# A graph layer and an LSTM layer on one core: the first 10,000 edges as products of summed weights with 80 support rows kept in SBUF, and ten gathered tiles a place instead of twelve

## The chip, the core and the metric

One NeuronCore of a Trainium2 chip runs the whole program. Its engines are TensorE (PE, with its weight loads shown as PEld), VectorE (DVE), ScalarE (ACT), GpSimd (POOL) and SyncE (SP), and 16 DMA engines move data between HBM and SBUF. Each engine works through its own queue in order, and they wait for each other on semaphores. The metric is the device time of one execution in microseconds, and less is better.

## What is computed

Two residual layers follow each other on x, 6250 nodes by 256 features. The first is a graph layer over 100,000 edges (sorted by `dst`), and the second is an LSTM over the nodes, with a gated sum over the nodes behind it.

```python
support  = einsum('ni,oi->no', layernorm(x), W_weight) + W_bias     # 6250 x 256
messages = support[dst] * edge_weight[:, None]                      # 100000 x 256
x = x + segment_sum(messages, src, num_segments=6250)
h = lstm(layernorm(x))                                              # one sequence of 6250 steps, 256 wide
w = argmax(h @ W_lin.T + b_lin) * h;  inc = cumsum(w)
x = x + 2.0 * h + (inc - w) * fw_att + (inc[-1] - inc) * bw_att
```

`dst` is drawn as 6250 times the square of a uniform number and then sorted, so small values are frequent and stand first: the first 10,000 edges name support rows 0 to 60 alone. `src` is uniform.

## The kernel before

**The layout.** The nodes are cut into 125 segments (`SEGS`) of 50 nodes (`SEGL`). A *place* is a position inside a segment, so one step of the LSTM handles 125 nodes at once, one of each segment. The first half of the program sorts the edges by place, computes `support`, and stores it in HBM as `support_scratch`. The sorted edges form *tiles* of 128 edges that belong to one place. A tile costs three operations:

- GpSimd gathers the 128 support rows of the tile from HBM with one indirect DMA into a slot of `ring` (a part of `big_a`), in `gather_place` (L573), by row numbers that ACT copied to `stg_g`.
- VectorE writes the tile's one-hot matrix, 128 edges by 125 segments with the edge weight in it, in `onehot` (L1180), four tiles ahead.
- TensorE multiplies the two into one of four PSUM banks, in `place_tile` (L1793), and VectorE adds the bank onto the place's rows of x, in `add_tile` (L1186). Which rows these are comes from `table`, whose entries `blocks` loads into registers of VectorE's sequencer (L1189).

**The stages.** 224 tiles are done while the edges are still being sorted (up to about 600 us of the profile). The other tiles are done in the *place stage*. It is a row of *turns* that each engine runs through as `place(it, q)`. Turn h = 2·it + q does `PACE` = 12 tiles, scales place h - 3 (layer norm), and runs the LSTM step for place h - 4. Tiles are in turns 2 to 50 (49 x 12 = 588 = `RUN`), and turns 51 and 52 have none. Then the LSTM runs alone (L1825, the same recurrence again from a better start), with the output sums beside it.

**The order inside a turn** is written out by hand on each engine. TensorE does tiles 0 and 1, then tiles 2 to 5 each behind a quarter of the 32 input projections (`project_input`, L1812), then tiles 6 to 9 with the 32 products of the recurrence between them (`product`, L1819), then tiles 10 and 11, then two transposes of the next scaled input (L1801). The profile shows an fp32 product of this size as two instructions, so a quarter is 8 matmul rows. VectorE does, for each tile n, `hot(n)` (the one-hot of tile n + 4) and `add(n)`, with the pieces of the layer norm (L1256 to L1320) and of the cell between them: `products` (L1327, L1329), `state` (L1335), `hidden` (L1340). It loads six table entries before tile 0 and six behind tile 5.

**What holds back what.** A product waits for its gather, for its one-hot, and for the addition four tiles back, which frees its PSUM bank. A gather waits, once in four (`PARTIAL`), for the product eight tiles back (`LOOK`). An addition waits for its product.

Of the kernel before, what the change touches and what calls it, by code (L numbers as in the profile page):

```python
# [6 lines left out]
P = 128  # L7
# [8 lines left out]
CC = 20  # L16
# [9 lines left out]
TILES = (EP * CC * CHUNKS + NB * (P - 1)) // P  # L26
# [3 lines left out]
RUN = 588  # L30
REST = TIL[1] - RUN
TMAX = max(TIL)
RECS = tuple(-(-t // P) for t in TIL)
RROWS = -(-(TILES * P // BLK + GRP * P) // P) * P
# [4 lines left out]
PACE = 12  # L39
WIDE = 2 * PACE  # L40
AHEAD = 4
HOTS = 8
PSR = 4
# [3 lines left out]
LAG, FIRST = 3, 2  # L47
# [14 lines left out]
INDEX_AT = 400  # L62
EPS = 1e-5
# [3 lines left out]
def build(nc, A, out, slow_sweeps=SEGS, tol=TOL):  # L67
# [14 lines left out]
    with ExitStack() as ctx:  # L82
# [15 lines left out]
        chunk_c = sb("chunk_consts", [CHUNKS, 5 * CHUNKS + 2])  # L98
        earlier, first, both, half, col_pair = (chunk_c[:, i * CHUNKS:(i + 1) * CHUNKS] for i in range(5))
        first_p = chunk_c[:, 5 * CHUNKS:5 * CHUNKS + 1]  # L100
        my_pair = chunk_c[:, 5 * CHUNKS + 1:5 * CHUNKS + 2]
# [109 lines left out]
        rect = at(flat_a, 11136, P, -(-TMAX // P), 2 * P)  # L211
        spread = at(flat_c, 1024, CHUNKS, SUPERS, 2, BB)
# [71 lines left out]
        gat = [sem(f"gathered{i}") for i in range(RING)]  # L284
        gat2 = [sem(f"gathered_by_place{i}") for i in range(WIDE)]
# [50 lines left out]
        o_v = sem("outputs_done")  # L336
        segt = sem("segment_totals_ready")
# [51 lines left out]
        def _(sp):  # L389

            def load_edges_of(tile, name, loaded):
                for a, b in PARTS:
                    sp.dma_start(tile[a:b, :], A[name].rearrange("(p c) -> p c", p=EP)[a:b, :]).then_inc(loaded, 16)
# [42 lines left out]

            def store_pair(i, to):
# [53 lines left out]
        def _(pool):  # L491
# [130 lines left out]
        def _(act):  # L622
# [179 lines left out]
            def place(it, q, w=0):  # L802
# [3 lines left out]
                if h > LAG + 1:  # L806
                    tanh_c(u - 1, 1 - q, 1)
# [1228 lines left out]
```

## Time and profile before

| | |
|---|---|
| three timed runs | 1674.13, 1678.54 and 1686.15 us, median 1678.54 |
| the profiled execution, its own span | 1678.9 us |
| busy in it: PE, PEld, DVE, ACT, POOL | 83%, 72%, 78%, 37%, 66% |
| mean granted TensorE clock | 0.945 |
| place stage (first to last addition of turns 2 to 50) | 604.72 to 1338.84 us |
| indirect gathers: of tiles before the place stage, of places | 224, 588 |

In a row of the trace an instruction group is shown as engine, line, operation, written tile, read tiles and count. A number in brackets is the time in which the engine stood idle before it, with what ended that. "issue" there is time in which the engine waited for nothing that the profile shows. The completion of a gather is often not seen as a releaser, and a wait for it then counts as "issue".

### The profile page before, as it was taken

What the parts mean: (1) busy time and instruction counts of PE and PEld (TensorE: products, weight loads), DVE (VectorE), ACT (ScalarE), POOL (GpSimd) and SP (SyncE); (2) the same over time, 40 slices, a digit from 0 to 9 for tenths busy, and PEclk for the clock granted to TensorE, in tenths of its full rate; (3) what the DMA queues carried; (4) which work ended last, traced back from release to release, by engine and by line L of the source; (5) the groups of instructions that cost most, each with busy time, mean ns of one, the idle gap of its engine ahead of it and who ended that gap; (6) DMA issues with size and microseconds to landing.
All of it is one profiled execution on the core that took longest, in us unless ns stands there. A gap on an engine that the chain in (4) does not pass through costs nothing.

```text
span 1678.9 us, 35611 instructions
## 1 busy us (share of the span) xinstructions
PE 1396.6 (83%) x9305; PEld 1206.7 (72%) x9305; DVE 1305.0 (78%) x3956; ACT 625.7 (37%) x2098; POOL 1101.8 (66%) x1165
## 2 busy tenths in 40 slices
PE   6688767877787759888889888888888889999991
PEld 3557665666676638777777777777777788999991
DVE  8799959999999867777777777777777744666666
ACT  0626630000000003333334333333433467777770
POOL 0226637777777777777777777777777600588884
PEclk9799977999999969999999999999999999999996
DMA  9211113334333334444444444444444334444434
GB/s 223 54 49 42 22 17 100 89 87 138 95 88 87 88 100 130 137 146 129 153 131 129 153 128 153 130 128 153 129 138 144 116 126 122 125 124 119 119 110 154
DMA packets 64189, 193.28 MB, mean 115 GB/s; under 512 B 21473, under 2 KB 22853, under 8 KB 63261
## 3 DMA queue, kind: packets, MB, share of 16 engines
q0 software_dynamic: 45232, 108.65, 23.6%
q1 hardware_dynamic: 18904, 84.00, 15.9%
q8 instruction: 23, 0.38, 0.1%
q14 instruction: 30, 0.25, 0.0%
HBM read 151.39 MB, written 41.04 MB: 115 GB/s over the span
## 4 chain that ended last, share of the span: by engine, by line
PE 51%; DVE 14%; issue 12%; DVEq 5%; ACT 1%; POOL 1%; DMA 1%; ACTq 0%; POOLq 0%
PE bank L1825 13%; PE bank L1793 13%; PE bank L1812 8%; PE bank L1750 5%; PE bank L1819 5%; PE bank L1719 5%; DVE big_c L1180 3%; DVE big_a L1129 3%; DVEq L1189 3%; DVE big_b L1186 2%; DVEq L1180 1%; DVE big_a L1535 1%; DVE big_a L1124 1%; PE bank L1855 1%; PE bank L1856 1%
## 5 line engine op out<-in xcount | busy, mean ns | idle before, releaser
L573 POOL DMA_INDIRECT big_a<-support_scratch,stg_g x588 | 563.0, 958 | 180.5 <-issue 143.3
L1793 PE MATMUL bank<-big_a,big_c 128*125 128x256 f32 x1176 | 362.9, 398 | 86.6 <-issue 58.3
L1186 DVE TENSOR_TENSOR big_b<-big_b,bank 125x256 f32 x812 | 338.8, 417 | 93.2 <-PE bank L1793 80.8
L1180 DVE TENSOR_SCALAR big_c<-consts_sb,listed 128x125 f32<-128x125 f32 x812 | 296.5, 366 | 37.1 <-issue 19.9
L1793 PEld LDWEIGHTS bank<-big_a,big_c 128*125 128x125 f32 x1176 | 180.5, 191 | 146.2 <-DVE big_c L1180 83.4
L527 POOL DMA_INDIRECT big_a<-support_scratch,stg_g x224 | 214.3, 957 | 73.6 <-issue 56.2
L1825 PE MATMUL bank<-big_c 128*128 128x125 f32 x2048 | 256.9, 280 | 4.6 <-DVE big_c L1340 4.6
L1825 PEld LDWEIGHTS bank<-big_c 128*128 128x128 f32 x2048 | 241.3, 191 | 15.5 <-issue 7.2
L1812 PEld LDWEIGHTS bank<-xt,w_ih 128*128 128x128 f32 x1600 | 207.9, 192 | 15.9 <-ACT xt L634 3.7
L1819 PEld LDWEIGHTS bank<-big_c 128*128 128x128 f32 x1600 | 209.0, 192 | 10.8 <-ACT bank L748 0.5
L1812 PE MATMUL bank<-xt,w_ih 128*128 128x125 f32 x1600 | 210.3, 275 | 2.6 <-ACT xt L634 2.5
L1819 PE MATMUL bank<-big_c 128*128 128x125 f32 x1600 | 209.8, 275 | 0.1
L1750 PE MATMUL bank<-big_a,big_c 128*125 128x256 f32 x448 | 139.9, 448 | 75.1 <-DVE big_b L1186 67.0
L1719 PEld LDWEIGHTS bank<-big_a,big_c 125*128 125x128 f32 x1480 | 184.6, 205 | 21.3 <-DVE big_a L1129 10.1
L1719 PE MATMUL bank<-big_a,big_c 125*128 125x128 f32 x1480 | 184.3, 287 | 16.3 <-DVE big_a L1129 8.4
L1750 PEld LDWEIGHTS bank<-big_a,big_c 128*125 128x125 f32 x448 | 85.4, 213 | 118.9 <-DVE big_c L1180 82.5
L740 ACT ACTIVATE pr<-bank,gate_bias 128x125 f32<-128x125 f32 x400 | 113.3, 367 | 89.1 <-PE bank L1812 88.3
L787 ACT ACTIVATE big_c<-big_c 128x125 f32<-128x125 f32 x228 | 70.3, 309 | 164.8 <-DVE big_c L1335 162.4
L508 POOL TENSOR_TENSOR pr<-pr,b_gnn 125x256 f32<-125x256 f32 x50 | 61.5, 1249 | 102.8 <-ACT pr L644 102.8
L694 ACT CAST stg_g<-listed 128x12 uint32 (+3 forms) x77 | 14.4, 190 | 302.0 <-PE bank L1750 238.4
L780 ACT ACTIVATE big_c<-bank 128x250 f32<-128x250 f32 x100 | 38.0, 380 | 225.3 <-PE bank L1819 225.3
L590 POOL TENSOR_TENSOR listed<-listed 125x256 f32<-125x256 f32 x50 | 36.5, 729 | 125.0 <-DVE listed L1472 124.8
(272 smaller groups left out, 1982.3 us busy)
## 6 DMA issues: line engine op xcount, KB each, us to landing
big_c<-gate_input_scratch SPq DMA_DIRECT2D x64, 508.0 KB, 3.6
gate_input_scratch<-pr SPq DMA_DIRECT2D x25, 1016.0 KB, 4.6
big_a<-support_scratch,stg_g POOLq DMA_INDIRECT x812, 2.8
support_scratch<-pr SPq DMA_DIRECT2D x12, 448.0 KB
big_b<-in_x SPq DMA_DIRECT2D x2, 1904.0 KB
out<-big_a SPq DMA_DIRECT2D x2, 1456.0 KB
big_b<-in_x SPq DMA_DIRECT2D x1, 1792.0 KB
out<-big_a SPq DMA_DIRECT2D x1, 1344.0 KB
```

The lines of the kernel that those rows point to most:

```text
L527: pool.indirect_dma_start(out=ring[:, s, :], out_offset=None, in_=sup_d, in_offset=bass.IndirectOffsetOnAxis(ap=stg_g[:, q, j:j + 1], axis ...
L573: pool.indirect_dma_start(out=ring[:, s, :], out_offset=None, in_=sup_d, in_offset=bass.IndirectOffsetOnAxis(ap=stg_g[:, q, n:n + 1], axis ...
L740: ins = nc.scalar.activation(gate_in[q][:, 4 * x + c, 2:XW], bank[2 + x][:, c * SEGS:(c + 1) * SEGS], ACT.Identity, bias=bias[:, 4 * x + c ...
L787: nc.scalar.activation(act_c[:, x, :], c_s[:, 1 - q, x, :], ACT.Tanh).then_inc(a_c[x], 1)
L1180: V.tensor_scalar(oneh[:, s % HOTS, 0:SEGS], iota[:, 0:SEGS], src_of[:, ds(t, 1)], w_of[:, ds(t, 1)], ALU.is_equal, ALU.mult).then_inc(oh_ ...
L1186: V.tensor_tensor(at, at, bank[4 + s % PSR][0:SEGS, 0:D], ALU.add).then_inc(added, 1)
L1719: ins = mm(bank[b][:, 0:2 * NPOS], slots_home(k, q)[:, c, :], col_v[:, q, c, :, :].rearrange("p v n -> p (v n)"), start=q == 0 and c == 0, ...
L1750: mm(bank[4 + s % PSR][0:SEGS, 0:D], oneh[:, s % HOTS, 0:SEGS], ring[:, s % RING, :], start=True, stop=True).then_inc(prod, 1)
L1793: mm(bank[4 + s % PSR][0:SEGS, 0:D], oneh[:, s % HOTS, 0:SEGS], ring[:, s, :], start=True, stop=True).then_inc(prod, 1)
L1812: ins = mm(bank[2 + x][:, c * SEGS:(c + 1) * SEGS], w_ih[:, k, g:g + P], xt[:, q, k, 0:SEGS], start=k == 0, stop=k == 1)
L1819: return mm(bank[b + x][:, c * SEGS:(c + 1) * SEGS], w_hh[:, k, g:g + P], h_s[:, q, k, :], start=False, stop=True, skip_group_check=True)
L1825: return mm(home, w_hh[:, k, g:g + P], h_s[:, q, k, :], start=False, stop=True, skip_group_check=True)
```

## The change

The edges are laid out anew, so that the first 10,000 of them fill the last four of the 40 chunks that are sorted. They get two tiles of 128 records for each place (`HOTP` = 2), and these 100 tiles are never gathered. The 80 first rows of `support` (`hot_sup`) are loaded into SBUF once. In each turn TensorE multiplies, for both tiles, a one-hot by support row (128 x 80, `hot_dst_1`) with a weighted one-hot by segment (128 x 125, `hot_seg_1`) and sums them in bank 5 (`sum_weights`). ACT copies the 80 x 125 sums to `hot_sum`, TensorE multiplies them with `hot_sup` into bank 4 (`hot_product`), and VectorE adds the result (`add_sum`). VectorE writes the four one-hots for a turn in the turn before (`next_sum`). The remaining edges fill 528 tiles of places, 510 of which are reserved for places with ten a turn, so turns 1 to 51 have tiles. What was a short repair for tiles that are left over has become a full second path that runs when a flag is set; it is also set if a place has more than 256 of the first edges or one of them names a row over 79.

```diff
-RUN = 588
+RUN = 510
-PACE = 12
+PACE = 10
-LAG, FIRST = 3, 2
+HELD = 5
+LAG, FIRST = 3, 1
+POSITION = (0, 2, 3, 4, 5, 6, 7, 9, 10, 11)
+ADDS_BEFORE = (-3, -1, 0, 1, None, 2, 3, 5, 6, 7)
...
+act.wait_ge(sum_p, g + 1)
+nc.scalar.copy(hot_sum[:, 0:SEGS], bank[5][0:HOTROWS, 0:SEGS]).then_inc(sum_r, 1)
...
+def add_sum():
+    dve.wait_ge(hot_pr, g + 1)
+    dve.wait_ge(added, before_us + 7)
+    V.tensor_tensor(at, at, bank[4][0:SEGS, 0:D], ALU.add).then_inc(added, 1)
...
+def hot_onehot(g, r, i, of):
+    if of == 0:
+        V.tensor_scalar(hot_seg_1[:, r, i, 0:SEGS], iota[:, 0:SEGS], hot_seg[:, ds(g * HOTP + i, 1)],
+                        hot_w[:, ds(g * HOTP + i, 1)], ALU.is_equal, ALU.mult)
+    else:
+        ins = V.tensor_scalar(hot_dst_1[:, r, i, :], iota[:, 0:HOTROWS], hot_dst[:, ds(g * HOTP + i, 1)], None,
+                              ALU.is_equal)
+        if i == HOTP - 1:
+            ins.then_inc(hot_r, 1)
...
+def sum_weights(g, r):
+    pe.wait_ge(hot_r, g + 1)
+    for i in range(HOTP):
+        ins = mm(bank[5][0:HOTROWS, 0:SEGS], hot_dst_1[:, r, i, :], hot_seg_1[:, r, i, 0:SEGS],
+                 start=i == 0, stop=i == HOTP - 1)
+    ins.then_inc(sum_p, 1)
+def hot_product(g):
+    pe.wait_ge(sum_r, g + 1)
+    mm(bank[4][0:SEGS, 0:D], hot_sum[:, 0:SEGS], hot_sup, start=True, stop=True).then_inc(hot_pr, 1)
...
 tile_of(0)
+sum_weights(g, r)
+if stepping:
+    project_input(u, q, 0, (0, 1))
 tile_of(1)
```

**TensorE at the start of a turn in the loop, before.** The rows are tile 0 (it multiplies `big_c`, the one-hot, with `big_a`, the gathered rows), tile 1, the first quarter of the projections (`w_ih`), and tile 2.

```order
L1791 REGISTER_ALU [waits onehot_ready]
L1793 MATMUL bank<-big_a,big_c 125x256 [waits tile_added,gathered_by_place0]
L1790 REGISTER_ALU
L1793 MATMUL bank<-big_a,big_c 125x256 [waits tile_added,gathered_by_place1,onehot_ready]
L1806 ISA
L1808 REGISTER_ALU [waits transposed2_ready]
L1812 MATMUL bank<-xt,w_ih 128x125 [waits gate_input_ready0]
L1812 MATMUL bank<-xt,w_ih 128x125 x3
L1790 REGISTER_ALU
L1793 MATMUL bank<-big_a,big_c 125x256 [waits tile_added,gathered_by_place2,onehot_ready]
```

The same place after the change:

```order
L1936 MATMUL bank<-big_a,big_c 125x256 [waits tile_added]
L1944 REGISTER_ALU [waits hot_onehots_ready]
L1946 MATMUL bank<-big_c 80x125 [waits tile_added]
L1946 MATMUL bank<-big_c 80x125
L1967 REGISTER_ALU
L1969 REGISTER_ALU [waits transposed2_ready]
L1973 MATMUL bank<-xt,w_ih 128x125 [waits gate_input_ready0]
L1973 MATMUL bank<-xt,w_ih 128x125 x3
L1929 REGISTER_ALU
L1935 REGISTER_ALU [waits gathered11,onehot_ready]
L1936 MATMUL bank<-big_a,big_c 125x256 [waits tile_added]
```

The two products of the weight sums (L1946) stand between tile 0 and all projections of the turn, behind a wait for `hot_onehots_ready`. Tile 1 now comes behind the first quarter of the projections.

**VectorE at the end of a turn, before.** The rows are the last one-hot and addition, `hidden` of the first half, and `products` of the second half; the next turn starts with the table load.

```order
L1335 TENSOR_TENSOR big_c<-big_c 128x125 [waits state_products_ready0]
L1180 ISA [waits tile_product_done]
L1180 TENSOR_SCALAR big_c<-consts_sb,listed 128x125
L1184 REGISTER_ALU
L1186 ISA [waits tile_added,tile_product_done]
L1186 TENSOR_TENSOR big_b<-big_b,bank 125x256
L1340 TENSOR_TENSOR big_c<-big_c 128x125 [waits tanh_c_done0]
L1327 TENSOR_TENSOR big_c<-big_c 128x125 [waits act_i_f_done1]
L1329 TENSOR_TENSOR big_c<-big_c 128x125 [waits tanh_g_done1]
L1189 ISA
L1189 TENSOR_LOAD table
```

The same place after the change:

```order
L1415 TENSOR_TENSOR big_c<-big_c 128x125 [waits state_products_ready0]
L1445 REGISTER_ALU
L1446 REGISTER_ALU [waits tile_product_done]
L1448 ISA [waits tile_added]
L1448 TENSOR_TENSOR big_b<-big_b,bank 125x256
L1543 ISA
L1543 TENSOR_SCALAR big_c<-consts_sb,big_c 128x125
L1420 TENSOR_TENSOR big_c<-big_c 128x125 [waits tanh_c_done0]
L1546 ISA
L1546 TENSOR_SCALAR big_c<-consts_sb,big_c 128x80
L1407 TENSOR_TENSOR big_c<-big_c 128x125 [waits act_i_f_done1]
L1409 TENSOR_TENSOR big_c<-big_c 128x125 [waits tanh_g_done1]
```

The last one-hot of the weight sums for the next turn (L1546, 128x80), which counts `hot_onehots_ready` up, is the third last instruction of VectorE's turn.

## Rows read from the trace of the kernel before

**Rows 1.** Windows: from:to, length, busy us (instructions) of each engine, clock, DMA.

```profile
0.00:603.00 603.00, 450.57 (x2573) 360.81 (x2573) 543.43 (x895) 128.13 (x397) 362.31 (x333) 0.89 0.33 84
...
655.00:1335.00 680.00, 601.73 (x4044) 526.90 (x4045) 509.19 (x2162) 262.71 (x898) 515.93 (x539) 1.00 0.44 138
```

**Rows 2.** Lines, 655 to 1335 us: group, count | busy, mean | idle before.

```profile
L573 POOL DMA_INDIRECT big_a<-support_scratch,stg_g x539 | 516.1, 957 | 164.3 <-issue 130.2 <-PE bank L1793 32.0 <-ACT stg_g L694 2.1
L1793 PE MATMUL bank<-big_a,big_c 128*125 128x256 f32 x1080 | 329.1, 392 | 78.6 <-issue 55.1 <-DVE big_c L1180 22.3
L1186 DVE TENSOR_TENSOR big_b<-big_b,bank 125x256 f32 x540 | 225.4, 417 | 75.7 <-PE bank L1793 72.3 <-issue 0.3
```

**Rows 3.** Timeline, TensorE in two turns: start us, us, group, idle before.

```profile
1049.68 0.67 PE L1793 MATMUL bank<-big_a,big_c 128*125 128x256 f32 x2 [1.48 <-issue]
...
1056.78 0.60 PE L1793 MATMUL bank<-big_a,big_c 128*125 128x256 f32 x2
1057.21 1.05 PE L1812 MATMUL bank<-xt,w_ih 128*128 128x125 f32 x8
1058.10 0.60 PE L1793 MATMUL bank<-big_a,big_c 128*125 128x256 f32 x2
```

**Rows 4.** Timeline, VectorE in the same two turns.

```profile
1050.48 0.42 DVE L1186 TENSOR_TENSOR big_b<-big_b,bank 125x256 f32 x1 [1.68 <-PE bank L1793]
...
1054.52 0.35 DVE L1180 TENSOR_SCALAR big_c<-consts_sb,listed 128x125 f32<-128x125 f32 x1 [0.90 <-issue]
...
1058.36 0.42 DVE L1186 TENSOR_TENSOR big_b<-big_b,bank 125x256 f32 x1
...
1059.22 0.42 DVE L1186 TENSOR_TENSOR big_b<-big_b,bank 125x256 f32 x1
1061.13 0.15 DVE L1302 TENSOR_SCALAR rstd<-sums 125x1 int32<-125x1 int32 x1 [1.49 <-issue]
...
1065.72 0.27 DVE L1335 TENSOR_TENSOR big_c<-big_c 128x125 f32<-128x125 f32 x1
1065.92 0.33 DVE L1180 TENSOR_SCALAR big_c<-consts_sb,listed 128x125 f32<-128x125 f32 x1
1066.17 0.40 DVE L1186 TENSOR_TENSOR big_b<-big_b,bank 125x256 f32 x1
1066.51 0.27 DVE L1340 TENSOR_TENSOR big_c<-big_c 128x125 f32<-128x125 f32 x1
1066.70 0.27 DVE L1327 TENSOR_TENSOR big_c<-big_c 128x125 f32<-128x125 f32 x1
...
1067.67 0.35 DVE L1180 TENSOR_SCALAR big_c<-consts_sb,listed 128x125 f32<-128x125 f32 x1 [0.50 <-PE bank L1793]
```

**Rows 5.** Timeline, LSTM stage: a write by VectorE, the product behind it.

```profile
1449.45 0.29 DVE L1340 TENSOR_TENSOR big_c<-bank,big_c 128x125 f32<-128x125 f32 x1 [0.37 <-ACT big_c L787]
...
1449.95 4.00 PE L1825 MATMUL bank<-big_c 128*128 128x125 f32 x32
```

**Rows 6.** Line L1189, the table load, whole program: ns min/median/max, first, last.

```profile
L1189 DVEq TENSOR_LOAD <-table x126: 594/810/2470, 257.7 to 1331.6; - x126
```

**Rows 7.** Chain of waits, the load behind tile 5: start us, us.

```profile
1043.85 1.41 DVEq L1189
```

**Rows 8.** Timeline, VectorE: first addition of turns 2, 3, 4, last of all.

```profile
604.72 0.42 DVE L1186 TENSOR_TENSOR big_b<-big_b,bank 125x256 f32 x1 [0.41 <-PE bank L1793]
...
614.71 0.41 DVE L1186 TENSOR_TENSOR big_b<-big_b,bank 125x256 f32 x1
...
628.79 0.41 DVE L1186 TENSOR_TENSOR big_b<-big_b,bank 125x256 f32 x1
...
1338.84 0.42 DVE L1186 TENSOR_TENSOR big_b<-big_b,bank 125x256 f32 x1 [0.40 <-PE bank L1793]
```

**Rows 9.** Timeline, TensorE in the turns without tiles: their projections.

```profile
1348.36 3.84 PE L1812 MATMUL bank<-xt,w_ih 128*128 128x125 f32 x32 [1.04 <-ACT xt L634]
...
1357.33 3.84 PE L1812 MATMUL bank<-xt,w_ih 128*128 128x125 f32 x32 [1.04 <-ACT xt L634]
```

More of the change, by code:

```diff
@@ L97, in build @@
         ident, iota, before, shift, ones = (consts[:, i, :] for i in range(5))
[L98 to L101, printed above, removed]
+        chunk_c = sb("chunk_consts", [CHUNKS, 6 * CHUNKS + 5 + 2 * BB])
+        earlier, first, both, half, col_pair, cold = (chunk_c[:, i * CHUNKS:(i + 1) * CHUNKS] for i in range(6))
+        first_p, my_pair, cold_p, hot_p, over = (chunk_c[:, 6 * CHUNKS + i:6 * CHUNKS + i + 1] for i in range(5))
+        hot_at, hot_n = (chunk_c[:, 6 * CHUNKS + 5 + i * BB:6 * CHUNKS + 5 + (i + 1) * BB] for i in range(2))
         number_i = sb("pair_numbers_i", [CHUNKS, CHUNKS + 1], i32)
@@ L283, in build @@
         gst = sem("gather_rows_staged")
-        gat = [sem(f"gathered{i}") for i in range(RING)]
-        gat2 = [sem(f"gathered_by_place{i}") for i in range(WIDE)]
+        gat = [sem(f"gathered{i}") for i in range(WIDE)]
         ln2 = sem("place_scale_steps")
@@ L435, in _ @@
                 sp.dma_start(tile[:, :, :], A[name].rearrange("(k p) f -> p k f", p=P)).then_inc(load_w, 16)
+            sp.wait_ge(scat, scattered(SUPERS))
+            sp.dma_start(rect_hot, rec_tiles[HOTAT:HOTAT + HOTT, :]).then_inc(rec_hot, 16)
+            for q in range(2):
+                sp.wait_ge(st0[q], SUPPORT_STORES[q])
+            sp.dma_start(hot_sup, sup_d[0:HOTROWS, :]).then_inc(load_hot, 16)
             def store_pair(i, to):
@@ L1449, in _ @@
                     place(it, q, SEGL - LEAD)
-            for q in range(2):
-                place(turning, q)
-            with dve.Fori(turning + 1, ENDING) as it:
+            for it in range(turning, turned_to + 1):
+                for q in range(2):
+                    place(it, q)
+            with dve.Fori(turned_to + 1, ENDING) as it:
                 for q in range(2):
@@ L1661, in _ @@
             mm(bank[2][0:CHUNKS, P // 2:P // 2 + BB], first, cnt, start=True, stop=True)
-            mm(bank[2][0:CHUNKS, P:P + BB], ones[0:CHUNKS, 0:CHUNKS], cnt, start=True, stop=True)
+            mm(bank[2][0:CHUNKS, P:P + BB], cold, cnt, start=True, stop=True)
             mm(bank[2][0:CHUNKS, 2 * P:2 * P + BB], both, cnt, start=True, stop=True)
```

291 lines of the change are left out of this document (207 added, 84 removed).

## The prediction

> **What bounds the kernel now.** I read the stages first, then the waits in the long one. The edges are sorted until about 603 us, and the change touches little there. The place stage runs from the first addition of turn 2 at 604.72 to the last addition at 1338.84 [rows 8]. In 680 us of it PE is busy 602 us, DVE 509, POOL 516, ACT 263, with the TensorE clock at its full level, 1.00 of 2.4 GHz [rows 1]. None of these shares is 100%, so it is the pace that tells. GpSimd makes 539 gathers in these 680 us, 516.1 busy and 164.3 idle, and 130.2 of the idle time is "issue", which is no wait for another engine [rows 2]. One gather thus takes (516.1 + 164.3) / 539 = 1.262 us, and 12 take 15.15 us, a turn. Only 34 us of its idle time, 0.06 us a gather, are waits for PE and ACT. TensorE waits 55.1 us for something that the profile does not show [rows 2]; the gap of 1.48 us in front of one tile's product is such a wait [rows 3], and a gather that had not landed fits it. VectorE waits 72.3 us for these products [rows 2]. Now the place stage goes at the pace of the gathers.
>
> How fast would the others be without that? In the turn from 1054.52 to 1067.67 VectorE waits for no product, apart from 0.50 us at its end that coincide with a table load: 13.15 us for 12 tiles [rows 4]. TensorE's minimum is smaller. A tile takes 1057.21 - 1056.78 = 0.43 us and a quarter of the projections 0.89 us (to the next tile at 1058.10), and the recurrence has four such parts as well [rows 3]. That makes 12 x 0.43 + 8 x 0.89 + 0.22 for the transposes (as two of the 8 in a quarter) = 12.5 us.
>
> **The change, engine by engine, a turn.** GpSimd: two gathers less, 10 x 1.262 = 12.6 us. TensorE: two tiles less (-0.87), the product with `hot_sup` (+0.43, one of a tile's size), and the weight sums, half the rows of a quarter (+0.44): 12.5 us as before. ScalarE: one copy more, on an engine busy 263 of 680 us [rows 1]. The trace has no such copy alone; between nothing and 0.5 us it is hidden, since the sums are wanted only by tile 4, four projections later. VectorE: a one-hot costs 1066.17 - 1065.92 = 0.25 us, an addition 1066.51 - 1066.17 = 0.34 [rows 4]. Two of each go (-1.18), one addition and four one-hots come (+1.34): 13.3 us.
>
> So by throughput a turn would fall to 13.3 us. **But the change also closes a chain.** TensorE's products of the weight sums stand in front of all projections of a turn and wait for a one-hot that VectorE writes as the third last instruction of the turn before. Queued behind that wait are the projections and tiles 1 to 4, and VectorE can't pass its addition of tile 4 without them. I go once round, with t = 0 where VectorE starts that last one-hot:
>
> - VectorE to TensorE: in the LSTM stage the product at 1449.95 follows the write it waited for, started at 1449.45, by 0.50 us [rows 5].
> - Weight sums 0.44, first quarter 0.89, then three steps of tile and quarter, 1.32 each (1056.78 to 1058.10) [rows 3]: tile 4 starts at 0.50 + 0.44 + 0.89 + 3.96 = 5.79.
> - Its addition starts 0.80 later, as the addition at 1050.48 does behind the product at 1049.68 [rows 3, 4]: 6.59.
> - VectorE from there. Before, from the addition of tile 4 at 1058.36 to `state` at 1065.72 it takes 7.36 us [rows 4]. After, the same stretch holds one addition less (-0.34), one one-hot less (-0.25) and two one-hots of the sums more (+0.50): 7.27. The table load is in both: 1.91 us from the addition at 1059.22 to 1061.13, of which the load is 1.41 [rows 4, 7]. It now stands behind tile 4.
> - From `state` to the last one-hot: 0.20, an addition 0.34, a one-hot 0.25, `hidden` 0.19 (1066.51 to 1066.70) [rows 4]: 0.98.
>
> Together 6.59 + 7.27 + 0.98 = 14.84 us a turn. VectorE's own way from t to the addition of tile 4 is shorter: 1058.36 - 1054.52 = 3.84, plus 0.97 from 1066.70 to 1067.67 and 0.25, 5.1 us [rows 4]. So it waits some 1.5 us a turn for tiles 3 and 4, and TensorE stands about 2.3 us in front of the weight sums. What goes away as a wait for gathers comes back here. 14.84 exceeds 13.3, 12.6 and 12.5, so it sets the turn.
>
> **The load's size is the unknown in it.** Before, six entries are loaded, from an even place in the table; after, five, half of the loads from an odd one. The trace has nothing of that shape. Its loads take from 0.59 us upwards with a median of 0.81, and 1.41 behind tile 5 [rows 6, 7]. I keep 1.41, the row from the same spot. At 0.6 the turn would be 14.0 us; if the new start costs as much more as lies between 0.81 and 1.41, 15.4 us. The Trainium skill ("DMA: Bandwidth & Descriptors", Latency and other measured facts) puts the floor of a `tensor_load` at about 600 ns. By that floor alone the turn would be 14.0 us and the time about 1645 us; the shortest loads here agree, the ones behind tile 5 do not.
>
> **The sum**, against the profiled 1678.9 us, which is the median of the three runs (1678.5) to within 0.4 us:
>
> - Turns 5 to 50, 46 of them: 14.84 for 15.15, -14.3.
> - Turn 51 gets tiles: 14.84 for the 8.97 us of a turn without them (1348.36 to 1357.33) [rows 9], +5.9.
> - Turn 1 is new. Turn 2, which has tiles alone, takes 614.71 - 604.72 = 10.0 us [rows 8]; with two tiles less and the sums' work more, by the prices above +0.16, about 10.1.
> - Turns 2 to 4: +0.1 in turn 2. Turn 3 takes 628.79 - 614.71 = 14.1 now [rows 8], with gathers as its pace; without that, 10.1 and the layer norm, some 12.5, -1.6. Turn 4 I take at 14.3 for 15.1, -0.8. Together -2.3.
> - Ahead of turn 1: some 15 small operations more on VectorE, each waiting for the one in front. Such an operation costs between 0.15 and 0.3 us (the smallest in a row lasts 0.15 [rows 4]), and some are hidden; then six to unpack the new records, four more one-hots (1.0), and a third transfer in front of the first operation. Bounds 1.5 and 7; I take 4.5.
>
> -14.3 + 5.9 + 10.1 - 2.3 + 4.5 = +3.9, so 1683 us. Every 0.1 us in the turn is 4.7 us here.
>
> **The rivals.**
>
> - *No chain, VectorE's throughput sets the pace*: 13.3 us a turn, 47 x 1.54 = 72 less, 1611 us. For it: the products of the sums are small, and some slack may be hidden from me, if the stretch of VectorE shortens. Against it: the order of both queues, which fixes every step above. The Trainium skill ("Perfetto Trace Analysis", Identifying the Most-Contended Engine) would have the most occupied engine relieved first, and by occupancy TensorE is that here, which the change does not relieve.
> - *Chain with cheap loads*: at 0.6 us a load 14.0 us a turn, 47 x 0.81 = 38 less, 1645 us. For it, the shortest and the median load; against it, the place in the table.
> - *The other side, dearer loads*: if a start at an odd entry costs 0.6 us more, 15.4 us a turn, 1711 us. It decides from 15.1 us, +0.27 in a turn, since there the time is 1% over. For it: the load behind tile 5 is dearer than the one at a turn's start, though both take six entries, so the start or the surroundings count.
> - *The gathers still pace*, since 10 take 12.6: it would give no less than VectorE's 13.3 and no more than 14.84, so the chain hides it.
> - *The change does not do what it says*: with the second path the time would be several times longer. Counted from the inputs, a place has at most 237 of the first edges (256 fit), they name rows up to 60 (80 fit), and the cold tiles of each place end at least four tiles within the limit. Under 1 in 100.
>
> **How the numbers follow.** The likeliest case is the chain at 14.5 to 15.1 us, with 0.5: 1667 to 1696 us, 1683 in its middle. Dearer loads or other extra steps on the chain 0.22, cheap loads 0.13, no chain 0.13, the rest 0.02. The range has to hold 8 in 10: it takes in the cheap loads and the dearer ones, 1640 to 1712, and leaves out the case without a chain. Under about 1% a measurement of this kernel can't be told from no change, so the bounds are 1662 and 1695. Faster: 0.26 from the two quick cases and a little of the main one, 0.28. Slower: 0.22 and the upper end of the main one, 0.27. Same: 0.45.
>
> **What would show it.** Right: additions evenly 14.8 us a turn apart; TensorE idle some 2 us in front of the products of the weight sums, released by VectorE's last one-hot (80 wide); VectorE waiting for the products of tiles 3 and 4; no gather late, and GpSimd waiting for TensorE some 2 us a turn. The load behind tile 4 shows its size directly. Wrong: weight sums that start without a gap, a turn near 13.3 us, or gaps of TensorE of the "issue" kind in front of gathered tiles.

## The result, and the profile after

The changed kernel takes 1661.5 us, the median of four runs (1658.7 to 1662.8). The kernel before took 1677.6 us beside it (four runs, 1674.1 to 1686.2). The ratio is 0.990, with a 95% interval from 0.987 to 0.993. So the change saves 16 us, 1.0%; the interval leaves out 1, so it is a gain, if a small one. The forecast was 1683 us, slightly more than before. The time lies in the range from 1640 to 1712, but the sign was wrong.

The profiled execution of the kernel after has a span of 1658.7 us, against 1678.9 before. These are 600 us of its place stage (window, its length, PE, PEld, DVE, ACT and POOL busy with their numbers of instructions, then the granted clock, the DMA share and GB/s).

```profile
700.00:1300.00 600.00, 538.77 (x3816) 485.36 (x3814) 476.29 (x2040) 245.26 (x871) 401.02 (x418) 1.00 0.41 128
```

GpSimd has become the engine with time to spare: 67% busy, where it was 76% in [rows 1]. TensorE's share has hardly risen, 90% for 88%. The groups of instructions of the same stretch answer to [rows 2]: busy time and mean ns of one, then the idle time in front of them and what ended it.

```profile
L630 POOL DMA_INDIRECT big_a<-support_scratch,stg_g x418 | 401.9, 962 | 199.3 <-issue 108.3 <-PE bank L1936 82.8 <-ACT stg_g L753 8.2
L1936 PE MATMUL bank<-big_a,big_c 128*125 128x256 f32 x830 | 238.0, 385 | 4.6 <-DVE big_b L1448 3.1 <-issue 1.5
L1448 DVE TENSOR_TENSOR big_b<-big_b,bank 125x256 f32 x415 | 173.6, 418 | 41.8 <-PE bank L1936 37.6 <-issue 0.2
L1946 PE MATMUL bank<-big_c 128*80 128x125 f32 x164 | 26.6, 285 | 55.2 <-DVE big_c L1546 55.2
```

No gathered tile comes late any more: the "issue" time in front of TensorE's tiles, 55.1 us before [rows 2], is 1.5 us. GpSimd waits 82.8 us for TensorE, 2.0 us a turn. In return TensorE waits 55.2 us in front of the weight sums (L1946), in each of the 41 turns of the stretch, for VectorE's 80-wide one-hot (L1546). The forecast named exactly this wait, but at 2.3 us a turn, where it is 1.35. Here is the turn on TensorE:

```profile
996.47 0.65 PE L1946 MATMUL bank<-big_c 128*80 128x125 f32 x4 [1.54 <-DVE big_c L1546]
996.96 1.06 PE L1973 MATMUL bank<-xt,w_ih 128*128 128x125 f32 x8
...
1007.54 1.03 PE L1936 MATMUL bank<-big_a,big_c 128*125 128x256 f32 x4
...
1010.90 0.65 PE L1946 MATMUL bank<-big_c 128*80 128x125 f32 x4 [1.12 <-DVE big_c L1546]
```

and on VectorE (start, duration; L1448 adds a tile, L1367 is the first operation behind the table load, L1415 is `state`, L1546 writes the 80-wide one-hots):

```profile
1001.33 0.42 DVE L1448 TENSOR_TENSOR big_b<-big_b,bank 125x256 f32 x1 [0.46 <-PE bank L1936]
...
1002.64 0.42 DVE L1448 TENSOR_TENSOR big_b<-big_b,bank 125x256 f32 x1 [0.44 <-PE bank L1936]
1004.22 0.15 DVE L1367 TENSOR_SCALAR tmp<-sums 125x1 f32<-125x1 f32 x1 [1.16 <-issue]
...
1008.37 0.42 DVE L1448 TENSOR_TENSOR big_b<-big_b,bank 125x256 f32 x1
...
1009.53 0.28 DVE L1415 TENSOR_TENSOR big_c<-big_c 128x125 f32<-128x125 f32 x1
...
1010.51 0.26 DVE L1546 TENSOR_SCALAR big_c<-consts_sb,big_c 128x80 f32<-128x80 f32 x1
```

From one L1946 to the next is 1010.90 - 996.47 = 14.43 us, and the turns of the stretch are even. VectorE waits in front of tiles 3 and 4, as foreseen (0.90 us here, 1.5 in the forecast). What is not as foreseen is the length, 14.43 us and not 14.84.

### The profile page after: what moved, and what is told of

Read it like the earlier page. It is cut to its first block, busy times and chain, and to the rows that moved or that the text cites. A ratio compares the mean times of both kernels' runs of the same rounds, so it can differ in the third digit from the quotient of the medians.

```text
span 1658.7 us, 36173 instructions
## 1 busy us (share of the span) xinstructions
PE 1387.2 (84%) x9451; PEld 1213.6 (73%) x9451; DVE 1328.6 (80%) x4070; ACT 630.2 (38%) x2150; POOL 1027.9 (62%) x1087
## 4 chain that ended last, share of the span: by engine, by line
PE 51%; DVE 17%; issue 8%; DVEq 5%; POOL 1%; ACT 1%; DMA 1%; POOLq 0%; ACTq 0%
PE bank L1986 13%; PE bank L1973 11%; PE bank L1936 8%; PE bank L1888 5%; PE bank L1980 5%; PE bank L1851 4%; DVE big_b L1448 3%; DVE big_a L1204 3%; DVEq L1264 2%; PE bank L1946 2%; DVE big_c L1546 1%; DVE big_c L1407 1%; DVE big_a L1665 1%; DVE big_c L1420 1%; DVE big_a L1199 1%
## 5 line engine op out<-in xcount | busy, mean ns | idle before, releaser
L630 POOL DMA_INDIRECT big_a<-support_scratch,stg_g x510 | 490.1, 961 | 232.9 <-issue 131.4
L1936 PE MATMUL bank<-big_a,big_c 128*125 128x256 f32 x1020 | 296.2, 391 | 9.2 <-DVE big_b L1448 5.0
L583 POOL DMA_INDIRECT big_a<-support_scratch,stg_g x224 | 213.9, 955 | 75.7 <-issue 57.3
L1448 DVE TENSOR_TENSOR big_b<-big_b,bank 125x256 f32 x510 | 213.3, 418 | 55.4 <-PE bank L1936 50.6
L1536 DVE TENSOR_SCALAR big_c<-consts_sb,listed 128x125 f32<-128x125 f32 x510 | 180.3, 354 | 40.7 <-issue 35.4
L1888 PE MATMUL bank<-big_a,big_c 128*125 128x256 f32 x448 | 140.3, 449 | 77.8 <-DVE big_b L1261 68.7
L1851 PE MATMUL bank<-big_a,big_c 125*128 125x128 f32 x1480 | 182.8, 286 | 16.3 <-DVE big_a L1204 8.4
L1936 PEld LDWEIGHTS bank<-big_a,big_c 128*125 128x125 f32 x1020 | 163.2, 192 | 28.9 <-DVE big_b L1448 9.7
L1888 PEld LDWEIGHTS bank<-big_a,big_c 128*125 128x125 f32 x448 | 85.1, 213 | 122.2 <-DVE big_c L1255 86.7
L846 ACT ACTIVATE big_c<-big_c 128x125 f32<-128x125 f32 x228 | 70.3, 308 | 222.1 <-DVE big_c L1415 219.8
L753 ACT CAST stg_g<-listed 128x10 uint32 (+3 forms) x79 | 14.8, 189 | 298.3 <-PE bank L1888 242.3
L1261 DVE TENSOR_TENSOR big_b<-big_b,bank 125x256 f32 x224 | 93.2, 416 | 8.4 <-PE bank L1888 8.0
```

The source lines that it names most:

```text
L583: pool.indirect_dma_start(out=ring[:, s, :], out_offset=None, in_=sup_d, in_offset=bass.IndirectOffsetOnAxis(ap=stg_g[:, q, j:j + 1], axis ...
L630: pool.indirect_dma_start(out=ring[:, s, :], out_offset=None, in_=sup_d, in_offset=bass.IndirectOffsetOnAxis(ap=stg_g[:, r, n:n + 1], axis ...
L1261: V.tensor_tensor(at, at, bank[4 + s % PSR][0:SEGS, 0:D], ALU.add).then_inc(added, 1)
L1448: V.tensor_tensor(at, at, bank[4 + POSITION[n] % PSR][0:SEGS, 0:D], ALU.add).then_inc(added, 1)
L1536: V.tensor_scalar(oneh[:, s % HELD, 0:SEGS], iota[:, 0:SEGS], src_of[:, ds(t, 1)], w_of[:, ds(t, 1)], ALU.is_equal, ALU.mult).then_inc(oh_ ...
L1851: ins = mm(bank[b][:, 0:2 * NPOS], slots_home(k, q)[:, c, :], col_v[:, q, c, :, :].rearrange("p v n -> p (v n)"), start=q == 0 and c == 0, ...
```

## The experiments

Each kernel was run four times, ten times where its size was unsteady or small, and once where only loads are looked at. The kernel before, run beside them, took 1677.9 to 1680.2 us. Turns are counted between the additions of the sums, as their mean from 700 to 1300 us of the profiled execution, or to the end of the place stage where that comes sooner.

### Three of the one-hots earlier: is the chain there?

```
 better_guess(j, p, 0)
 next_sum(0, 0)
+next_sum(0, 1)
+next_sum(1, 0)
+next_sum(1, 1)
...
 hot(9)
-next_sum(0, 1)
...
 add(9, vals)
-next_sum(1, 0)
...
     hidden(u, q, 0)
-next_sum(1, 1)
```

> The changed kernel with the other three one-hots of the next place's sums moved up beside the first of them, ahead of the addition of the sums (some 4 us earlier in VectorE's order); the work is the same. Theory (a chain from the last of them through TensorE's weight sums, tiles 1 to 4 and back sets the turn): the chain opens, TensorE's idle time of 1.1 to 1.5 us in front of the weight sums goes, and the turn falls from 14.45 to VectorE's own 13.2 to 13.6 us, its waits for tiles 3 and 4 taken off. 47 turns by 0.85 to 1.25 is 40 to 59 us: 1603 to 1622 us. Rival (a turn is as long as the work on TensorE or VectorE, the order does not count): within 5 us of 1661.

Measured: 1637.3 us, 24 less than after; ratio to before 0.976 (0.974 to 0.978). The same work in another order gains, so order counts, and the wait in front of the weight sums is gone. But a turn takes 13.91 us in the mean, and not 13.2 to 13.6, and the time misses the 1603 to 1622 us expected. The next wait is in TensorE's rows, at the projections (L1972):

```profile
996.72 1.15 PE L1972 MATMUL bank<-xt,w_ih 128*128 128x125 f32 x8
...
1008.95 0.43 PE L1961 MATMUL bank<-consts_sb,xn 125*128 125x125 f32 x2 [0.52 <-DVE xn L1400]
...
1010.73 1.16 PE L1972 MATMUL bank<-xt,w_ih 128*128 128x125 f32 x8 [0.38 <-ACT xt L693]
```

and in ScalarE's rows of the same moment, the tanh of the cell state (L846) and behind it the copy of the input (L693):

```profile
1010.11 0.31 ACT L846 ACTIVATE big_c<-big_c 128x125 f32<-128x125 f32 x1 [1.80 <-DVE big_c L1415]
1010.33 0.35 ACT L693 COPY xt<-bank 128x250 f32<-128x250 f32 x1
```

The wait of 0.52 us in front of the transposes (L1961) does not count in this turn, since TensorE waits again behind it. The copy was ready to be made earlier, but it stands in ScalarE's queue behind a tanh that waits for VectorE's `state`. So there is a third way round: projections, tile 4, its addition, the table load, `state`, tanh, copy, projections. It takes 14.01 us here.

### The table aligned: what does the load cost, and is it on the path?

```
+link(V.tensor_copy(spaced_t[0:1, 0:16 * RUN // 10].rearrange("p (x e) -> p x e", e=8)[:, :, 0:5],
+                   table[0:1, TFROM[1]:TFROM[1] + RUN].rearrange("p (x e) -> p x e", e=5)))
...
-return blocks(first + (TFROM[1] + n), PACE // 2) if n < count else None
+return blocks(g * 16 + n // 5 * 8, PACE // 2, spaced_t) if n < count else None
```

> The changed kernel with the table of places copied once into groups of 8 words with five used, so that every load of five entries begins at a multiple of 8. If the start in the table is what makes a load take 1.18 us and not 0.60, both loads of each turn take 0.60. The chain goes through the one behind tile 4, so the turn is 14.45 - 0.58 = 13.87 us and the time 47 x 0.58 = 27 us less, about 1634. If the place of the load in the program makes it dear (a load behind tile 4 and not its start), nothing changes: 1661. If loads are cheaper but the turn does not follow, the chain is wrong.

The loads of the kernel after, and of this one (least, median and greatest ns):

```profile
L1264 DVEq TENSOR_LOAD <-table x84: 586/1183/1210, 699.6 to 1299.8; - x84
```

```profile
L1265 DVEq TENSOR_LOAD <-table_by_places x83: 585/590/601, 701.1 to 1294.5; - x83
```

Every load now takes 0.59 us, so the start in the table makes it dear and not its place in the program. Yet the time is 1664.2 us (ratio to before 0.991, 0.988 to 0.994) and the turn 14.48 us: nothing is gained. (The copy of the table is not what hides a gain: VectorE spends 0.4 us on it, ahead of the stage, and the turn itself is no shorter.) VectorE now waits at other tiles. These are the additions of tiles 7 and 8:

```profile
1000.79 0.42 DVE L1449 TENSOR_TENSOR big_b<-big_b,bank 125x256 f32 x1 [0.27 <-PE bank L1939]
...
1002.11 0.42 DVE L1449 TENSOR_TENSOR big_b<-big_b,bank 125x256 f32 x1 [0.25 <-PE bank L1939]
```

So what I expected if the turn didn't follow, "the chain is wrong", is too short: the chain is real, but a second one stands beside it. From the weight sums on TensorE has no gap until tile 8, 1007.54 - 996.47 = 11.07 us in the kernel after. The addition of tile 8 can start 0.80 us later, VectorE goes from it to the last one-hot in 1010.51 - 1008.37 = 2.14 us, and TensorE follows 0.39 us behind: 14.40 us. In the kernel after the two ways, through tile 4 with the load and through tile 8 without it, differ by 0.03 us. To shorten one brings nothing. Moving the one-hots cuts both, since both end in them.

### Three more one-hots, ahead of the last one or behind it

```
+aside = sb("one_hots_aside", [P, 3, HOTROWS])
...
+if summing:
+    for n in range(3):
+        V.tensor_scalar(aside[:, n, :], iota[:, 0:HOTROWS], hot_dst[:, ds(g * HOTP, 1)], None, ALU.is_equal)
 next_sum(1, 1)
```

That is the one with the three ahead. In the other the same lines stand behind `next_sum(1, 1)`.

> The changed kernel with three more 80-wide one-hots a turn on VectorE (0.17 us each, written to a spare place, read by nobody) directly ahead of the last one-hot of the sums. Theory of the chain: all 0.51 us lie on it, 47 turns by 0.51 is +24 us, 1685. Rival (throughput of VectorE): also +24.

> The same three one-hots directly behind the last one-hot of the sums instead of ahead of it. Theory of the chain: they lie beside TensorE's weight sums and first projections, where VectorE later waits some 0.9 us for tiles 3 and 4, so they are covered: within 3 us of 1661, and these waits get shorter by 0.5 us in all. Rival (throughput of VectorE): +24 us, 1685, as with the three ahead.

Behind it, they cost nothing: 1660.4 us, with VectorE busy for 20 us more in the stretch (496.75 for 476.29):

```profile
700.00:1300.00 600.00, 541.38 (x3815) 485.08 (x3814) 496.75 (x2165) 244.93 (x870) 397.51 (x418) 1.00 0.41 128
```

I had expected the waits for tiles to cover all of these 20 us, and they cover a part. VectorE's idle time in front of its additions that ends with a product falls from 37.6 to 32.7 us, and most of the rest goes from the idle time in front of the tiles' one-hots, 30.8 us in the kernel after and 16.0 here.

Ahead of it, the same three cost 91 us: 1752.9 us, and not the 24 expected. This pair is the clearest proof of the chain, since only the place differs. The size has a second cause. A few turns take 14.9 to 15.0 us, which is 14.43 + 0.51 as the chain has it, but most take 16.5 to 17.0. TensorE's rows at two turns, both behind a wait for the last one-hot (L1550):

```profile
1013.06 0.65 PE L1950 MATMUL bank<-big_c 128*80 128x125 f32 x4 [1.93 <-DVE big_c L1550]
1013.54 1.06 PE L1977 MATMUL bank<-xt,w_ih 128*128 128x125 f32 x8
...
1045.12 1.01 PE L1950 MATMUL bank<-big_c 128*80 128x125 f32 x4 [2.23 <-DVE big_c L1550]
1045.92 1.91 PE L1977 MATMUL bank<-xt,w_ih 128*128 128x125 f32 x8
1047.63 1.06 PE L1940 MATMUL bank<-big_a,big_c 128*125 128x256 f32 x2
```

The same eight products take 1.06 us in one turn and 1.91 in the other. The stretches of these moments show why (the third number from the end is the granted clock):

```profile
1014.00:1016.00 2.00, 2.00 (x18) 1.92 (x17) 1.31 (x6) 0.55 (x3) 0.18 (x1) 1.00 0.17 51
...
1046.00:1048.00 2.00, 2.00 (x10) 1.96 (x10) 0.33 (x2) 0.56 (x3) 0.00 (x0) 0.50 0.07 27
...
1050.00:1052.00 2.00, 2.00 (x19) 1.95 (x17) 1.39 (x7) 1.46 (x5) 1.39 (x3) 1.00 0.23 66
```

Behind 2.23 us of idleness the clock is at its lower level, 1.2 GHz, and the path stretches by 1.5 to 2 us until it is back. The Trainium skill ("TensorE: Matmul & The Clock Gate", What's actually happening) says that the reduced clock is the default and that activity lifts it; this trace agrees, with the clock at 0.50 behind the idle time and at 1.00 again later in the same turn.

### One more one-hot ahead

```
+aside = sb("one_hots_aside", [P, 3, HOTROWS])
...
+if summing:
+    V.tensor_scalar(aside[:, 0, :], iota[:, 0:HOTROWS], hot_dst[:, ds(g * HOTP, 1)], None, ALU.is_equal)
 next_sum(1, 1)
```

> The changed kernel with one more 80-wide one-hot (0.17 us) directly ahead of the last one-hot of the sums, where three made turns of 14.95 us at TensorE's full clock and of 16.5 to 16.9 us with it at its lower level behind the longer gap. Theory (the chain sets the turn, and the clock is what made three cost 92 us): the gap in front of the weight sums stays near that of the changed kernel, the clock stays at its full level, and the turn is 14.43 + 0.17 = 14.60: 47 x 0.17 = 8 us, 1669. Rival (an operation there costs in proportion to what three cost): +31, 1692.

Measured: 1674.5 us, the median of ten runs that lie far apart (1669.6 to 1689.5). The lowest of them are what the chain gives, 1669. The profiled execution is the longest of the ten, and it shows both in one:

```profile
700.00:1000.00 300.00, 267.78 (x1905) 242.21 (x1905) 236.37 (x1023) 123.20 (x433) 201.01 (x205) 1.00 0.40 124
1040.00:1300.00 260.00, 231.69 (x1552) 208.14 (x1551) 196.29 (x843) 100.78 (x354) 160.03 (x170) 0.95 0.39 122
```

From 730 to 1020 us most turns are 14.60, to the hundredth what 14.43 + 0.17 makes. From then on many take 16.3 us, with the clock at the lower level behind the wait. The length of the wait in front alone does not decide it: 1.3 us was followed by the lower clock in some turns of this kernel, and in the kernel with the aligned table waits of up to 1.86 us were all followed by the full one. So 0.2 us a turn on top of the kernel after is enough for TensorE's idle time to cost more than itself in some executions. What exactly sets the edge stays open.

### Two more gathers, and the kernel before eased elsewhere: did the gathers pace it?

```
+for n in range(2):
+    if not isinstance(it, int) or it > 0:
+        pool.wait_ge(more_l[n], it * 32 + (q * 16 - 16))
+        pool.sem_inc(go, 1)
+    pool.indirect_dma_start(
+        out=more[:, n, :], out_offset=None, in_=sup_d,
+        in_offset=bass.IndirectOffsetOnAxis(ap=more_i[:, n:n + 1], axis=0)).then_inc(more_l[n], 16)
 for n in range(tiles_at(it, q)):
     s = r * PACE + n
```

> The changed kernel with two more gathers a turn on GpSimd, into a spare place that nobody reads: 12 a turn as before the change, all else as after it. Theory (a gather costs 1.262 us whatever else happens, 12 of them paced the kernel before): the turn goes from 14.43 to 15.15 us, 47 x 0.72 = 34 us more, 1695; gaps of the issue kind come back in front of gathered tiles. Rival (the kernel before was paced by VectorE and TensorE, and the gathers only followed): within 5 us of 1661.

Measured: 1716.7 us, ratio to before 1.022 (1.019 to 1.024). The turn is 15.1 us with turns between 14.4 and 16.6, which is in the mean the 15.15 of 12 gathers. TensorE waits for the gathers' data again, now named as such:

```profile
L641 POOL DMA_INDIRECT big_a<-support_scratch,stg_g x399 | 381.2, 955 | 121.6 <-issue 107.5 <-PE bank L1950 8.8 <-ACT stg_g L766 5.2
L1950 PE MATMUL bank<-big_a,big_c 128*125 128x256 f32 x797 | 239.4, 394 | 56.9 <-DMA big_a<-support_scratch,stg_g 40.6 <-DVE big_b L1461 12.2 <-DVE big_c L1549 2.8
```

The 22 us above the expected 1695 lie ahead of the stretch: the first added gather waited for its row numbers, so that the first sum was added at 620.9 us and not at 611.7, and the next three turns, with little other work in them, took 15.3, 15.3 and 17.8 us where they had taken 9.4, 11.2 and 13.2. (Of the 9 us, 4 are not the gather's: VectorE began to unpack the last sorted edges at 601.2 us in this execution and at 597.0 in that of the kernel after.)

The other half of the question is the kernel before with two edits, the aligned table (eight words for six entries) and ScalarE's copy ahead of its tanh:

```
-return blocks(first + (TFROM[1] + n), PACE // 2) if n < count else None
+return blocks(place * 16 + n // 6 * 8, PACE // 2, spaced_t) if n < count else None
...
-    tanh_c(u, q, 0)
 if h >= LAG:
     copy_input(j, 1 - q, h < LAG + 2)
+if h > LAG:
+    tanh_c(u, q, 0)
```

> The kernel before the change with two edits that the best version has: its table copied into groups of 8 words with six used, and ScalarE's copy of xt ahead of the tanh. Theory (the gathers pace it, 12 x 1.26 = 15.15 us a turn): nothing moves, 1679 within 5 us, and VectorE waits longer for the products of tiles. Rival (loads and the order of ScalarE paced it, the gathers only followed): 47 x 0.5 = 24 us less or more.

Measured: 1677.8 us beside 1677.9, ratio 1.0003 (0.9992 to 1.0015) over ten runs, although all its loads now take 0.81 us. Its gathers keep the pace of [rows 2], (513.9 + 163.9) / 538 = 1.26 us each. VectorE's waits for tiles have grown from 72.3 to 82.1 us, and the "issue" time in front of TensorE's tiles from 55.1 to 67.5:

```profile
L574 POOL DMA_INDIRECT big_a<-support_scratch,stg_g x538 | 513.9, 955 | 163.9 <-issue 129.2 <-PE bank L1798 33.2 <-ACT stg_g L695 1.5
L1798 PE MATMUL bank<-big_a,big_c 128*125 128x256 f32 x1085 | 330.5, 392 | 76.1 <-issue 67.5 <-DVE big_c L1182 7.4
L1188 DVE TENSOR_TENSOR big_b<-big_b,bank 125x256 f32 x543 | 226.5, 417 | 84.6 <-PE bank L1798 82.1
```

### Both, and all ways opened

The early one-hots with the aligned table, the two diffs above together:

> The early one-hots and the aligned table together. Read from the two runs: with aligned loads alone the turn stayed at 14.4, since TensorE then works without a break from the weight sums to tile 8 (11.07 us), and the addition of tile 8 (+0.80), 2.14 us of VectorE to the last one-hot and 0.39 back make 14.40: a second way round, as long as the first. With early one-hots alone the turn was 13.98, on a third way: projections, tile 4, its addition, the load, `state` at 1009.79, ScalarE's tanh and its copy of xt behind it, projections at 1010.73. Theory of ways of nearly one length: this third one holds the load, so aligning it is now worth what it was not before: 0.58 us a turn, down to 13.4, 47 x 0.55 = 26 us less than 1637, about 1611. Rival (loads don't matter at all, or TensorE's work is reached at 14.0): 1637.

Measured: 1622.6 us, ratio to before 0.966 (0.964 to 0.968), turns of 13.52. The same alignment that brought nothing on the kernel after brings 15 us here, a good half of the 26 that I expected; TensorE still waits 0.5 us for the copy of xt in every second turn or so. VectorE waits for tile 4 in every turn and for tile 8 in about half of them, so the way through tile 8, which holds no load, is now as long as the one through tile 4. Here it is from projections (L1975) to projections, with the addition of tile 8 (L1449) and `state` (L1416):

```profile
1003.86 1.16 PE L1975 MATMUL bank<-xt,w_ih 128*128 128x125 f32 x8 [0.52 <-ACT xt L694]
...
1014.55 1.03 PE L1938 MATMUL bank<-big_a,big_c 128*125 128x256 f32 x4
1015.38 0.42 DVE L1449 TENSOR_TENSOR big_b<-big_b,bank 125x256 f32 x1
1016.37 0.28 DVE L1416 TENSOR_TENSOR big_c<-big_c 128x125 f32<-128x125 f32 x1
1017.37 1.15 PE L1975 MATMUL bank<-xt,w_ih 128*128 128x125 f32 x8
```

10.69 + 0.83 + 0.99 + 1.00 = 13.51 us. I had put the turn at 13.40, and so counted on more of the load's 0.58 us than this way leaves.

The best version keeps the aligned table, takes the one-hots from their old places to the front of the turn, and the copy ahead of the tanh:

```
 vals = blocks_from(0)
+next_sum(0, 0)
+next_sum(0, 1)
+next_sum(1, 0)
+next_sum(1, 1)
 hot(0)
...
-    tanh_c(u, q, 0)
 if h >= LAG:
     copy_input(j, 1 - q, h < LAG + 2)
+if h > LAG:
+    tanh_c(u, q, 0)
```

> All ways opened: the four one-hots of the next place's sums stand first in a turn, where VectorE waits 1.4 us with the early ones; the table is aligned; and ScalarE copies xt before the tanh for the first direction, so that the projections no longer wait for `state`. Theory: what is left is TensorE's own turn, which is 14.01 less its idle 0.52 + 0.38 of the turn read = 13.1 us; 47 x (14.43 - 13.1) = 63 less than 1661, about 1598 (1590 to 1605). Rival: another way of 13.4 or more (gathers at 12.6 are too short for one) keeps it at 1611.

Measured: 1586.2 us, ratio to before 0.943 (0.941 to 0.945), 75 us less than the kernel after. Turns are 12.64 and 13.07 us in alternation, 12.82 in the mean:

```profile
700.00:1230.00 530.00, 526.50 (x3800) 485.14 (x3799) 470.52 (x2023) 246.08 (x870) 396.24 (x415) 1.00 0.45 142
```

TensorE is busy for 526.5 of 530 us. Only here does its work set the turn. That is 12.7 us of work a turn, where I had read 13.1 from the kernel with the early one-hots; what the difference is made of I can't tell.

The same without the aligned table:

> The best version without the aligned table, so only two moves in the order of queues: the four one-hots at the start of a turn and ScalarE's copy ahead of the tanh. In the best version TensorE is 99.3% busy and VectorE waits for products only 0.13 us a turn, so VectorE's own work is nearly as long as TensorE's; dear loads add 0.3 (mean of the first ones) and 0.58 us to it: about 13.6 us a turn for 12.84, 47 x 0.75 = 35 us more than 1586, 1621. Rival (VectorE has slack there that the waits don't show): 1586.

Measured: 1623.0 us, ratio to before 0.968 (0.966 to 0.970), with turns of 13.2 and 14.3 in alternation, 13.61 in the mean. Here VectorE sets the turn: in front of its 411 additions of tiles between 700 and 1260 us it stands idle for 1.1 us in all. The load's price depends on its start, and where VectorE has no slack nearly all of it counts: 13.61 - 12.82 = 0.79 us a turn, for the 0.88 (0.3 + 0.58) by which its loads are dearer.

### What a load costs

45 loads, whose entries single copies then use, ahead of VectorE's end:

```
+for o in range(9):
+    for n in (2, 4, 5, 6, 8):
+        vals = blocks(TFROM[1] + o, n)
+        for v_ in vals:
+            ins = V.tensor_copy(seen[0:1, at_seen:at_seen + 1], acc[0:1, ds(v_, 1)])
+            at_seen += 1
```

> The changed kernel with 45 loads ahead of VectorE's end whose entries are all used (in single-entry copies): 2, 4, 5, 6 and 8 entries from each of nine places in a row, the first a multiple of 8. Those of before and after take 0.60 (8 from a multiple of 8, 5 from a multiple of 4), 0.81 (6 from a multiple of 4), 1.18 (5 from elsewhere), 1.41 us (6 from elsewhere). If the time follows place and number together, these four come back at these places, and the others between them; if something around the loads made them dear, all loads of one number are alike.

These are loads from a multiple of 4 that is none of 8, of 4, 6 and 8 entries, and from the entry behind it, of 5, 6 and 8:

```profile
L1265 DVEq TENSOR_LOAD <-table x1: 372/372/372, 1682.0 to 1682.0; - x1
...
L1265 DVEq TENSOR_LOAD <-table x1: 834/834/834, 1684.7 to 1684.7; - x1
...
L1265 DVEq TENSOR_LOAD <-table x1: 602/602/602, 1686.4 to 1686.4; - x1
...
L1265 DVEq TENSOR_LOAD <-table x1: 1181/1181/1181, 1690.7 to 1690.7; - x1
...
L1265 DVEq TENSOR_LOAD <-table x1: 1403/1403/1403, 1692.6 to 1692.6; - x1
...
L1265 DVEq TENSOR_LOAD <-table x1: 1844/1844/1844, 1694.9 to 1694.9; - x1
```

| entries | 2 | 4 | 5 | 6 | 8 |
|---|---|---|---|---|---|
| start at a multiple of 4 | 0.55 | 0.37 | 0.60 | 0.83 | 0.60 |
| any other start | 0.53 | 0.97 | 1.18 | 1.40 | 1.84 |

The table is of the last seven starts, which agree among themselves within 0.02 us; at the first two starts some loads are disturbed. From a multiple of 4, four more entries cost 0.23 us (0.60 for eight, 0.37 for four), as much as a single one more (0.60 for five), and from any other start each entry costs 0.22. This holds even where a multiple of 4 lies inside the load. It accounts for every size seen before and after: 0.60 for eight, 0.81 and 1.41 for six, 0.60 and 1.18 for five. The Trainium skill ("DMA: Bandwidth & Descriptors", Latency and other measured facts) gives a floor of about 600 ns for a `tensor_load`. This trace does not agree: four aligned entries take 0.37 us.

An earlier try at the same had loads whose entries nobody used:

> The changed kernel with 63 loads of table entries on VectorE ahead of its end, 2 to 8 entries at each of nine places in a row, from a multiple of 8 on; they lengthen the run by about their own time. If alignment makes the time: 0.60 us for up to 8 entries from a multiple of 8 and for up to 4 or 5 from a multiple of 4, about 1.2 otherwise. If the number of entries makes it: the time grows with it at every place alike.

It told nothing: the trace has no row of these loads, and the time is that of the kernel after, 1660.9 us.

## Why the prediction was wrong in its sign, and where it was right

**The step that failed** is a size, that of the table load on the chain ("I keep 1.41, the row from the same spot"). It measured 1.18 us, and with what stands around it makes 15 us of the 24 by which the sum was too long. The 4.5 us for small operations ahead of turn 1 make 5 more. Either correction takes the sum below the time before.

**What bounded the kernel before: right.** The gathers set the pace, at 1.262 us each. Easing VectorE and ScalarE left the time at 1.0003 of itself, and two gathers put back into the kernel after brought back 15.1 us a turn. This is a pace in the mean only: the first additions of the turns before lie about 13.1 and 17.2 us apart in alternation. The turn of 13.15 us from which I took VectorE's own time is one of the short ones, and what makes the alternation stays open.

**The chain: right in its mechanism, in its order and in where it waits.** The last one-hot, the weight sums, the projections with tiles 1 to 4 and the addition of tile 4 follow as told. A one-hot's time put ahead of the last one lengthens the turn by itself (14.60), behind it by nothing.

**The sizes on it: 0.41 us too much a turn.** By the forecast's own steps: VectorE to TensorE 0.39 (1010.51 to 1010.90) for 0.50; sums to tile 4 5.35 for 5.29; its addition 0.82 later for 0.80; from there to `state` 6.89 (1002.64 to 1009.53) for 7.27; to the last one-hot 0.98 for 0.98. The largest part is the table load, 1.58 us between the operations around it (1002.64 to 1004.22) where I kept 1.91; 0.23 of these 0.33 us are the load itself. The same step also has an 80-wide one-hot in it, 0.17 us where I priced 0.25. That was the step "I keep 1.41, the row from the same spot". The spot was not what made it dear. From a start that is no multiple of 4, five entries cost 1.18 and six 1.41. I had the hint in hand, loads of six entries at 0.81 and at 1.41 [rows 6, 7], and took it for a matter of surroundings. 46 turns at 14.44 and not 14.84 are 18.5 us (1314.67 - 650.58 = 664.1 for 682.6).

**The second way round: missing.** The rival "chain with cheap loads", 14.0 us a turn, could not have come true; the aligned table gave it cheap loads and stayed at 14.4 to 14.5. I had checked TensorE by its sum of work alone, 12.5 us. What had to be summed is its work from the weight sums to tile 8, and VectorE's from there to the last one-hot. By the rows of the kernel before, 0.50 + 0.44 + 8 x 0.89 + 8 x 0.43 + 0.80 = 12.30 as far as the addition of tile 8, and in the rows of after 2.14 more: 14.44. So 14.4 was a floor under the whole case with a chain, and a range for it would have begun there.

**Ahead of turn 1: 5 us too much.** I took 4.5 for new small operations. The first addition of a place comes at 604.09 us, in [rows 8] at 604.72: nothing was added. Two things I had not subtracted: the unpacking now works on 400 columns, no longer 478, and three copies for leftover tiles are gone. Here are the new unpacking and what it costs, from the first to the last operation of its own:

```profile
600.14 0.26 DVE L1553 COPY big_c<-bank 128x100 f32<-128x100 f32 x1
...
601.11 0.41 DVE L1559 CAST big_c<-big_c 128x100 f32<-128x100 int32 x1
```

That is 1.4 us, with four one-hots of 0.9 us behind it. From the start of the unpacking to the first addition VectorE takes 604.09 - 596.99 = 7.1 us after and 604.72 - 598.60 = 6.1 before, so 1.0 us was added there and the rest saved. The other 1.6 us came earlier, and need not be the change: in the profiled executions of all these kernels the unpacking starts anywhere from 595.8 to 604.6 us.

**Turns 1 to 4: right**, 650.58 - 604.09 = 46.5 us for 47.0. **The ends: right.** From the first addition of the last turn with tiles to the first product of the LSTM alone it is 41.2 us before (1327.08 to 1368.26) and 31.9 after (1314.67 to 1346.53), 9.3 apart, as the sum has it (15.15 + 8.97 - 14.84). Two small parts remain. The kernel before took 1327.08 - 643.76 = 683.3 us for turns 5 to 49, where I counted 681.8. And from the first product of the LSTM alone to the end it is 312.2 us after and 310.6 before, which I had not in the sum and can't attribute. Together: -18.5 for turns 5 to 50 after, -5.1 ahead of turn 1, -0.5 for turns 1 to 4, -1.6 and +1.6 for the two small parts. That is -24.1 us, and the profiled span, 1658.7, is 24.1 below the sum's 1682.8.

**The other side.** The dearer loads that I gave 0.22 were excluded: an odd start costs no more than one at 2 of 4. But I priced a longer chain as straight, 4.7 us for each 0.1 us a turn. The run with one more one-hot shows that this holds only while the clock stays up, and the three show 91 us for 24. At the 14.84 us that I forecast, with 2.3 us of TensorE idle in front of the sums, the clock would probably have fallen in many turns, and the kernel would have been slower than 1683. This is argued from the two runs on either side of 14.84 and not shown at it.

## What to carry to other kernels

When a throttled engine is relieved, look for every way round the turn and not only for the first one: for each queue in turn, sum from the wait to the last instruction that must follow it, and take the longest. The aligned table gained nothing on the kernel after, 15 us with the early one-hots and 37 us in the best version, once the ways beside it were open. So edits that cut the common piece of several ways (here: writing the next place's one-hots a whole turn ahead) come first. An edit that brings idle time to TensorE has to be priced with the clock at its lower level behind it as well.

## What the runs showed of the hardware that I had not expected

- A table load into registers on VectorE costs by groups: 0.37 us for four entries from a multiple of 4, 0.60 for eight, 0.60 for five, and from any other start 0.22 us for each entry (0.97 for four, 1.84 for eight).
- TensorE's clock fell behind waits of a length that the kernel after also has (1.3 us, where that one has 1.1 to 1.6). With 0.17 us more a turn, one execution ran 300 us at its full clock and then 260 us at 0.95 in the mean; with 0.51 us more, the stretch from 700 to 1300 us had 0.92, and the time rose by 91 us for 24 us of work.
- An 80-wide one-hot occupies VectorE for 0.17 us until the next one starts (603.18 to 603.35 us in the kernel after), where a 125-wide one takes 0.25 (602.93 to 603.18).
